# A state-space layer on one core: the first 64 tap columns are computed from repacked inputs

## The reference, cut to what matters

```
x = x + einsum('bct,bcd->bdt', x, weights[condition])         # 64 x 128 x 2048
K = 2 * real(einsum('hn,hnl->hl', Ct, exp(dtA * arange(2048))))  # 128 channels, 64 modes
y = irfft(rfft(x, 4096) * rfft(K, 4096))[..., :2048] + x * D     # causal convolution
x = x + y * (arange(2048) < length)
```

## Time and profile before

| | us |
|---|---|
| time, median of 3 runs | 1100.93 |
| profiled execution, its own time | 1104.8 |
| its span, first to last instruction | 1102.7 |
| TensorE busy in the span | 1003.3 |
| VectorE busy | 624.6 |
| ScalarE busy | 547.6 |
| GpSimd busy | 451.5 |

### The profile page before, as it was taken

The page is one execution under the profiler, slowest core; times in us unless marked ns, Lnnn a source line. Parts: engine busy times, 40 slices in busy tenths (PEclk is TensorE's granted clock), DMA queues, the critical chain, the costliest instruction groups (busy, mean ns, idle before and its releaser), DMA issues.

```text
span 1102.7 us, 24659 instructions
## 1 busy us (share of the span) xinstructions
PE 1003.3 (91%) x9478; PEld 743.9 (67%) x9478; DVE 624.6 (57%) x1518; ACT 547.6 (50%) x1163; POOL 451.5 (41%) x542
## 2 busy tenths in 40 slices
PE   6977789677757999999999999999999999999997
PEld 2322344223215888888888888888888888888886
DVE  6989920000003666666666666666666666666664
ACT  2634344343433555555555555555555555555553
POOL 3101043000203456556456456455455565564520
PEclk9999999999987999999999999999999999999999
DMA  9999999999989789999999899899999999999984
GB/s 338 415 425 421 425 422 420 384 423 425 423 308 318 186 222 220 235 222 233 216 224 229 227 228 222 227 227 223 228 228 226 224 222 234 220 229 227 223 205 116
DMA packets 220292, 305.18 MB, mean 277 GB/s; under 512 B 79938, under 2 KB 178626, under 8 KB 211986
## 3 DMA queue, kind: packets, MB, share of 16 engines
q1 hardware_dynamic: 219490, 302.37, 93.7%
q10 hardware_dynamic: 528, 1.05, 0.3%
q0 software_dynamic: 160, 0.20, 0.1%
HBM read 152.37 MB, written 134.41 MB: 260 GB/s over the span
## 4 chain that ended last, share of the span: by engine, by line
PE 68%; DMA 26%; ACT 3%; SPq 2%; issue 1%; DVE 0%; ACTq 0%
DMA u_scratch<-stage 25%; PE bank L476 23%; PE bank L482 15%; PE bank L441 13%; PE bank L427 10%; PE bank L453 6%; ACT stage L548 3%; PE bank L415 2%; DMA x_f<-in_x 1%; SPq L245 1%; SPq L212 0%; SPq L232 0%; SPq L239 0%; DVE o_sb L823 0%; DVE u_t L810 0%
## 5 line engine op out<-in xcount | busy, mean ns | idle before, releaser
L476 PE MATMUL bank<-toep,u_t 128*128 128x256 f16 (+1 forms) x3072 | 394.8, 247 | 0.0
L482 PE MATMUL bank<-g_sb,st_sb 128*128 128x256 f16 x1536 | 307.3, 274 | 0.0
L810 DVE SCALAR_TENSOR_TENSOR u_t<-bank,u_t 128x512 f16<-128x512 f32 x256 | 176.5, 689 | 216.7 <-ACT u_t L561 216.5
L415 PE MATMUL bank<-x_f,w_buf 128*128 128x512 f32 x512 | 237.2, 610 | 67.1 <-ACT stage L548 58.5
L476 PEld LDWEIGHTS bank<-toep,u_t 128*128 128x128 f16 x3072 | 280.5, 98 | 25.3 <-issue 0.4
L427 PE MATMUL bank<-ident,u_row 128*128 128x128 f32 x1024 | 279.9, 278 | 11.3 <-DMA u_row<-u_scratch 10.7
L569 ACT ACTIVATE st_sb<-bank 128x128 f16<-128x128 f32 x448 | 124.0, 277 | 294.3 <-PE bank L453 204.6
L815 DVE TENSOR_TENSOR st_sb<-bank,st_sb 128x128 f16<-128x128 f32 x448 | 130.7, 292 | 191.6 <-ACT st_sb L569 189.2
L415 PEld LDWEIGHTS bank<-x_f,w_buf 128*128 128x128 f32 x512 | 94.2, 193 | 205.7 <-issue 103.7
L823 DVE COPY_PREDICATED o_sb<-mask,u_row 128x512 f32<-128x512 uint8 x256 | 212.8, 831 | 16.9 <-issue 16.8
L548 ACT ACTIVATE stage<-bank 128x1024 f32<-128x1024 f32 x128 | 123.9, 1021 | 173.2 <-DMA u_scratch<-stage 160.7
(11 more groups left out here) (118 smaller groups left out, 475.5 us busy)
## 6 DMA issues: line engine op xcount, KB each, us to landing
x_f<-in_x SPq DMA_DIRECT2D x64, 1024.0 KB, 19.6
u_row<-u_scratch SPq DMA_DIRECT2D x128, 512.0 KB, 5.5
out<-o_sb SPq DMA_DIRECT2D x256, 256.0 KB, 3.8
u_scratch<-stage SPq DMA_DIRECT2D x60, 1024.0 KB, 17.7
toep<-k_scratch SPq DMA_DIRECT2D x64, 256.0 KB, 5.4
u_scratch<-stage SPq DMA_DIRECT2D x4, 896.0 KB, 10.9
gt_sb<-g_sb SPq DMA_TRANSPOSE x128, 4.7
u_scratch<-stage SPq DMA_DIRECT2D x4, 128.0 KB, 4.7
```

The lines of the kernel that those rows point to most:

```text
L415: last = pe.matmul(bank[:, 4 * (n % 2) + k, :], w_buf[n % XS][:, :], x_f[n % XS][:, k * 512:(k + 1) * 512], start=True, stop=True)
L476: pe.matmul(bank[:, y, col + tb * P:col + Q], lhs, t[:, h, b, 0:Q - tb * P], start=first, stop=False, skip_group_check=True)
L482: last = pe.matmul(bank[:, y, col:col + Q], st[:, h, a, gr * ROWS:(gr + 1) * ROWS], g[:, h, b, :], start=False, stop=(m == 2), skip_group_ ...
L810: dve.scalar_tensor_tensor(out=t[:, q // 2, q % 2, 1, :], in0=bank[:, 4 + q, :], scalar=US, in1=t[:, q // 2, q % 2, 0, :], op0=MUL, op1=SU ...
```

## The change

`toep` keeps its shape, but its first 64 columns no longer have zeros in the partitions 0 to 63: `fold_toeplitz` copies the taps of the partitions 64 to 127 there. A new tile `x_t`, two buffers, holds the inputs that belong to these columns: `first_half` copies the partitions 64 to 127 of the inputs' high half (part 0) into its partitions 64 to 127, and those of the low half (part 1) into its partitions 0 to 63. One product with `x_t` then forms high and low inputs at once. In `out_part` the three matmuls of a half block begin at column 64, and two matmuls of 64 columns with `x_t` (high and low taps) fill the first 64. VectorE does the three copies in its slot: the taps of pair c ahead of ("u", c + 1, 0), the inputs behind states 1 and 2. TensorE's first part waits for them (`s_tz`, `s_xt`) in place of the DMA's semaphore; VectorE waits for that. To make room, `turns_r` of the set-up shares the memory of `wide[3]`.

```diff
--- before.py
+++ after.py
@@ -106,7 +106,7 @@
         waves = sb("waves", [P, 2 * NS + 1, H], F32, making)
         turns = waves[:, NS:2 * NS, :]
         wide = [sb(f"wide{i}", [P, NS, H], F32, making) for i in range(4)]
-        turns_r = sb("turns_r", [P, NS, H], F32, making)
+        turns_r = wide[3]
         ex = [sb(f"ex{i}", [P, 2, H], F32, making) for i in range(3)]
         ex_i = sb("ex_i", [P, 2, H], I32, making)
         nat = [sb(f"nat{i}", [P, 2 * P], F32, making) for i in range(3)]
@@ -123,7 +123,7 @@
         lam_sb = [sb(f"lam_sb{i}", [P, 2, 2, 2, NM], F16, tables) for i in range(2)]
         toep = [sb(f"toep{i}", [P, 2, 2, Q], F16, tables) for i in range(4)]
         tables.close()
-        sb("making_bytes", [P, (2 * NS + 1 + 5 * NS + 2 * NS) * H + 4 * 2 * H + 3 * 2 * P + 4 * H], F32)
+        sb("making_bytes", [P, (2 * NS + 1 + 4 * NS + 2 * NS) * H + 4 * 2 * H + 3 * 2 * P + 4 * H], F32)
         k_lhs = sb("k_lhs", [P, H, 16], F32)
         tmp_t = sb("tmp_t", [P, 256], F32)
         p2 = sb("p2", [P, NS], F32)
@@ -132,6 +132,8 @@
             sb(n, [P, H], F32) for n in ("ai", "cr", "ci", "dec", "e_re", "omega", "cycles", "freq"))
         s_re, s_im, k_a, k_b, c_top = (sb(n, [P, H], F32) for n in ("s_re", "s_im", "k_a", "k_b", "c_top"))
         k_zero = sb("k_zero", [P, 1], F32)
+
+        x_t = [sb(f"x_t{i}", [P, 2, 2, NG * ROWS], F16) for i in range(2)]
         k_head = sb("k_head", [P, 2, P], F16)
         k_body = [sb(f"k_body{k}", [16, 2, HT, 16], F16) for k in range(2)]
 
@@ -160,6 +162,7 @@
             sem(n) for n in ("s_gx", "s_gs", "s_gh", "s_g", "s_go", "s_lam"))
         s_gt = [sem(f"s_gt{i}") for i in range(2)]
         s_st, s_sth, s_stl = (sem(n) for n in ("s_st", "s_sth", "s_stl"))
+        s_xt, s_tz = sem("s_xt"), sem("s_tz")
         s_out, s_y, s_ov = (sem(n) for n in ("s_out", "s_y", "s_ov"))
 
         block = ctx.enter_context(nc.Block())
@@ -459,9 +462,10 @@
             def out_part(i, c, k, between):
                 h, gr, n = k // NG, k % NG, UN * i + c
                 u, g, t, st = u_t[c % 4], g_sb[c % 4], toep[c % 4], st_sb[c % 2]
-                y, col = 2 + (k // 2) % 2, (gr % 2) * Q
+                y, col, rows_ = 2 + (k // 2) % 2, (gr % 2) * Q, slice(gr * ROWS, (gr + 1) * ROWS)
                 if k == 0:
-                    pe.wait_ge(s_t[c % 4], 16 * (i + c // 4 + 1))
+                    pe.wait_ge(s_tz, n + 1)
+                    pe.wait_ge(s_xt, 2 * n + 2)
                 if k % 2 == 0:
                     wait(pe, s_y, 4 * n + k // 2 - 1)
                 if h == 0:
@@ -471,13 +475,15 @@
                 first = True
                 for tb in range(2):
                     for a in range(2):
-                        lhs = u[:, h, tb, a, gr * ROWS:(gr + 1) * ROWS]
                         for b in range(2 - a):
-                            pe.matmul(bank[:, y, col + tb * P:col + Q], lhs, t[:, h, b, 0:Q - tb * P],
-                                      start=first, stop=False, skip_group_check=True)
+                            pe.matmul(bank[:, y, col + tb * P + NM:col + Q], u[:, h, tb, a, rows_],
+                                      t[:, h, b, NM:Q - tb * P], start=first, stop=False, skip_group_check=True)
                             if first:
                                 between(2 * k)
                             first = False
+                    for b in range(2):
+                        pe.matmul(bank[:, y, col + tb * P:col + tb * P + NM], x_t[c % 2][:, h, tb, rows_],
+                                  t[:, h, b, 0:NM], start=False, stop=False, skip_group_check=True)
                 for m, (a, b) in enumerate(SPLIT):
                     last = pe.matmul(bank[:, y, col:col + Q], st[:, h, a, gr * ROWS:(gr + 1) * ROWS],
                                      g[:, h, b, :], start=False, stop=(m == 2), skip_group_check=True)
@@ -815,6 +821,23 @@
                 dve.tensor_tensor(out=state(st_sb[c % 2], 1, j), in0=new_state(j),
                                   in1=state(st_sb[c % 2], 0, j), op=SUB).then_inc(s_stl, 1)
 
+            def first_half(i, c, part):
+
+                n = UN * i + c
+                if part == 0:
+                    dve.wait_ge(s_ul, 4 * n + 4)
+                    wait(dve, s_out, 4 * (n - 1))
+                to = slice(NM, P) if part == 0 else slice(0, NM)
+                dve.tensor_copy(x_t[c % 2][to, :, :, :].rearrange("p h b r -> p (h b) r"),
+                                u_t[c % 4][NM:P, :, :, part, :].rearrange("p h b r -> p (h b) r")).then_inc(s_xt, 1)
+
+            def fold_toeplitz(i, c):
+
+
+                dve.wait_ge(s_t[c % 4], 16 * (i + c // 4 + 1))
+                dve.tensor_copy(toep[c % 4][0:NM, :, :, 0:NM].rearrange("p h a t -> p (h a) t"),
+                                toep[c % 4][NM:P, :, :, 0:NM].rearrange("p h a t -> p (h a) t")).then_inc(s_tz, 1)
+
             def overlay(i, c, v):
                 dve.wait_ge(s_y, 4 * (UN * i + c) + v + 1)
                 at = 4 * (c % 2) + v
@@ -829,14 +852,18 @@
                 u_lo(0, 0, q)
 
             def slot(i, c):
-                for what, of, k in (("s", c - 1, 7), ("u", c, 3), ("o", c - 2, 3), ("u", c + 1, 0), ("o", c - 1, 0),
-                                    ("s", c, 1), ("s", c, 2), ("s", c, 3), ("u", c + 1, 1), ("s", c, 4),
+                for what, of, k in (("s", c - 1, 7), ("u", c, 3), ("o", c - 2, 3), ("t", c, 0), ("u", c + 1, 0), ("o", c - 1, 0),
+                                    ("s", c, 1), ("x", c, 0), ("s", c, 2), ("x", c, 1), ("s", c, 3), ("u", c + 1, 1), ("s", c, 4),
                                     ("o", c - 1, 1), ("s", c, 5), ("u", c + 1, 2), ("s", c, 6), ("o", c - 1, 2)):
                     if has(i, of):
                         if what == "s":
                             state_lo(i, of, k)
+                        elif what == "t":
+                            fold_toeplitz(i, of)
                         elif what == "u":
                             u_lo(i, of, k)
+                        elif what == "x":
+                            first_half(i, of, k)
                         else:
                             overlay(i, of, k)
```

## The result

Twenty runs of the changed kernel took 1093.8 to 1103.06 us, median 1097.43; twenty of the kernel before, on the same chips, 1099.57 to 1107.35, median 1103.13. The ratio is 0.9951, 95% interval 0.9936 to 0.9967: 0.5% faster, some 5.5 us, where 13.9 us were forecast. The sign was right, and so were the pace of the new matmuls and the duration of the copies. The size was not: nearly half of TensorE's gain was lost in short gaps that the forecast put at nothing.

The account below looks back on a forecast made before the run. TensorE, busy 100% of the main loop, was taken as the bound: -21.7 us of matmuls + 7.8 us of stalls = -13.9 us from 1100.9, about 1087 us. Range 1078 to 1112 us, the forecast's own 1082 to 1094.

Parts of the forecast that it names:

- TensorE's part: Taps' matmuls in each part: 1024 columns in ten instructions for 1152 in six, 43 ns a part less, 21.7 us.
- state 3's stall: TensorE's wait before state 3's advance: no slack, only part 4's shortening between, 0.04 us a slot.
- The copies' own time: VectorE's three copies: 0.69 us for each inputs' copy, 0.23 us for the taps', 1.6 us a slot.
- The lock: VectorE's copies and GpSimd's table operations keep each other out of SBUF: 0.13 us stall a slot, 60 slots, 7.8 us.
- state 1: State 1, late behind the delayed taps' copy and overlay, makes TensorE stall 0.08 us a slot.
- The prediction's own sign of being wrong: Wrong if inputs' copies took over 1 us alone, or if state 3 rather than state 1 were the long wait.
- line 325 gets in ahead: Rival: GpSimd's line 325 claims before the second inputs' copy; state 3 stalls 0.6 us a slot, 1123 us; chance 0.11.
- No collision: Rival: copies do not take the lock, or cover is 0.13 us larger; 1079 us, or 1082; chance 0.20.
- The copies by elements: Rival: inputs' copies on VectorE take 1.23 us each, stalls of 0.7 us a slot, 1129 us; chance 0.08.
- the dear narrow matmuls: Rival: 64-column matmuls on TensorE cost 35 ns, the gain is gone, 1100 to 1105 us; chance 0.06.
- DMA: Rival: DMA saturates at share 0.96 and bounds the main loop, slot near 11.5 us, 1088 us; chance 0.09.
- The start of the loop: Pair 0's copies lie before 354 us under the wait for late stores and cost nothing; uncovered, under 2 us each.

Follow-up runs that it names:

- the combined kernel: Changed kernel with shared copy semaphore, no high-half wait (parts 0 to 3), taps' copy before overlay, state 3 before input quarter, later first transpose: ratio 0.9875, loop 701.9 us.
- TensorE's part alone, cleaned: Changed kernel without copies in the loop, without high-half wait (parts 0 to 3), state 3 before ScalarE's input quarter, later first transpose: ratio 0.9851, loop 697.0 us.
- one semaphore: Changed kernel with all three copies counting the same semaphore, four waits at the slot's first matmul instead of five: ratio 0.9948, loop 708.6 us.

## Why the prediction was wrong

- **TensorE's part: the step that failed.** "All three fit 0.417 ns a column plus 2.6 ns an instruction", so 43 ns a part and 21.7 us. The pace was right (29 ns a narrow matmul, 0.45 us a part), and over the loop the instructions alone are 21.0 us shorter. But the term went into the sum as if nothing stood between them. As the kernel stood TensorE's part gave 10.4 us, or 13 us when state 3's stall is counted with the stalls, as the prediction does. It was read inside a part, and nothing was put down for the slot's first matmul, which has to see its waits met behind six parts of dense narrow matmuls. Shown: one wait for the state's high half, implied by another, cost 4.7 us (705.6 to 700.9), and waits cost next to nothing behind the old matmuls (a fifth one 0.5 us, though mending them there gives up to 2.9). What in TensorE's front needs that time was not measured.
- **The copies' own time: right.** 687 to 692 ns against 0.69, 222 against 0.23 us; bytes decide, not elements. The Trainium skill (VectorE: DVE Perf Modes, section The perf-mode tier table) gives 693 ns for a copy of 2048 bf16 elements, and the 692 ns here agree.
- **The lock: right in its working, its sum right in size by luck.** The taps' copy took 1.03 us for 1.1, in the place forecast. But of the 7.8 us, state 1 was to bring nearly 5 and brought 2.1 us, since the gap at the slot's start hid most of it; once that was gone its stall came out at 0.136 us a slot for 0.08. State 3's small stall came as forecast (2.5 us), and without any copy (2.7 us). In state 1's place stood the long stalls of the rival below, 3.2 us, which the sum did not hold.
- **The prediction's own sign of being wrong came true:** state 3, not state 1, is the long wait, 5.7 us against 2.1.
- **The rival "line 325 gets in ahead"** happened in 4 of 60 slots, 0.6 us forecast, 0.8 us measured (3.2 us), not in all. The range allowed for it in a part of the slots, the sum did not; as a share of the slots it belonged there.
- **No collision** would have been -10.6 us in the loop (705.4). **The copies by elements, the dear narrow matmuls:** refuted. **DMA:** its share rose from 0.93 and 0.95 to 0.97 and 1.00, and the combined kernel was still faster by another 8 us of loop, so it was no bound.
- **The start of the loop:** the same for both within its scatter, as forecast.

The range began at 1078 and ended at 1112, and the forecast's own range ended at 1094; the median of the changed kernel, 1097, is 0.5% under that of before, not 1.3%. Put together for the loop: 21 us forecast for TensorE's matmuls, 13 got (10.4 + state 3's 2.7); 7.8 forecast for stalls, 6.7 came (that 2.7 and the copies' 709.6 - 705.6 = 4.0). The 6.4 us are the difference.

## What to carry to other kernels

An engine that is busy 100% has no gaps to read: when its work shrinks, look from start to start at the instructions that carry several semaphore waits, drop every wait that another implies, and expect the slack of each state to shrink with the work around it. Where two engines lock each other out, put a short copy between the other's operations, ahead of a long one of its own engine and not behind it: moving one copy of 0.22 us by one place took away a stall of 0.136 us in some 45 slots here, 6.3 us. Take obstacles away together as well as one by one, since each may hide the next. And where one profiled execution says 10 us and the timed runs say 5, believe neither number to the microsecond.

## What the runs showed that was not expected

- Waits that are already met cost next to nothing behind matmuls of 128 to 256 columns, and up to 0.2 us behind seven of 64 in a row and six more, in about every second slot.
- A matmul or its neighbour sometimes has no releaser for 0.3 to 1.7 us ("issue" in the row). In the combined kernel, in the middle of six matmuls of an advance:

```profile
600.86 0.19 PE L456 MATMUL bank<-st_sb,lam_sb 128*128 128x64 f16 x1
601.85 0.32 PE L456 MATMUL bank<-st_sb,lam_sb 128*128 128x64 f16 x5 [0.80 <-issue]
```

By my sums they cost the kernels with the narrow matmuls some 1.4 to 6.6 us in the loop, and those with the old matmuls at most 0.8 us.
- The places are not by chance. In the five kernels with narrow matmuls that leave out the wait for the high half, a wait of 0.45 to 1.02 us stands ahead of the very same matmul, the first of one late slot. TensorE's part alone, cleaned, then the combined kernel:

```profile
924.23 0.34 PE L477 MATMUL bank<-toep,u_t 128*128 128x192 f16 x2 [0.86 <-issue]
923.38 0.33 PE L477 MATMUL bank<-toep,u_t 128*128 128x192 f16 x2 [0.58 <-issue]
```

Four of the seven kernels with narrow matmuls that keep that wait have 0.52 or 0.53 us ahead of one and the same transpose (761.57 in the changed kernel, 759.35 with one semaphore), and none of the seven has a long wait at the place above. So the place goes with the instruction stream. That the instruction itself arrives late fits this, but it is a guess: it was not tried and stays open.
